# First attention and first mixture of a two-layer gated block: earlier start of block 0, ternary halves one step later, a written-out ending, 23 tiles and weight loads in pieces

## The reference, cut to what matters

```python
x = x + tanh(g_xattn[0]) * xattn0(layernorm(x), ctx, ctx)   # 16 heads of 16, softmax over 128 keys
x = x + tanh(g_ffn[0]) * ffn0(layernorm(x))
# xattn0: q = x Wq + bq; k = ctx Wk + bk; v = ctx Wv + bv; softmax(q k / 4) v Wo + bo
# ffn0: weights replaced by sign * row mean of |W| where |W| > half of that mean, else 0
#   shared expert:  silu(h sw1^T) sw2^T
#   routed expert:  the one of 8 experts with the largest router probability, times that probability
```

## Time and profile before

| | |
|---|---|
| median of three runs | 1084.05 us |
| the profiled execution, its own time | 1094.73 us |
| its span from the first to the last instruction | 1093.0 us |
| mean granted TensorE clock over the span | 0.938 |
| PE, DVE, ACT, POOL busy | 89%, 71%, 56%, 21% of the span |
| first attention | 0 to 210.7 us |
| routing and shared expert | 210.9 to 282.2 us |
| expert tiles | 282.5 to 363.2 us |
| second layer | from 363.3 us to the end |

### The profile page before, as it was taken

One profiled execution on the slowest core, in us unless ns is written; L12 is line 12 of the kernel. 1 busy time (PEld: TensorE's weight loads), 2 busy tenths in 40 slices (PEclk: granted clock), 3 DMA queues, 4 the chain that ended last, 5 costly groups with the idle time before them and its releaser, 6 DMA issues. The chain is left out here.

```text
span 1093.0 us, 22464 instructions
## 1 busy us (share of the span) xinstructions
PE 972.3 (89%) x8152; PEld 900.7 (82%) x8152; DVE 770.8 (71%) x1924; ACT 609.9 (56%) x1460; POOL 229.9 (21%) x289
## 2 busy tenths in 40 slices
PE   3899999777798579999999999999979999799992
PEld 2788887677687468999999999999968999698991
DVE  5788887664576677878777767766776777465655
ACT  3477775374597545555555555555537444565650
POOL 3534443005000342010100000010000000466631
PEclk9799998778899879999999999999999999899996
DMA  8511110002264220000000000003014000444417
GB/s 273 180 60 41 60 60 2 1 9 69 89 192 110 61 64 1 20 14 8 21 1 20 2 20 1 21 1 97 1 60 135 1 2 6 126 130 136 139 56 260
DMA packets 66044, 69.67 MB, mean 64 GB/s; under 512 B 14352, under 2 KB 56848, under 8 KB 65808
## 3 DMA queue, kind: packets, MB, share of 16 engines
q1 hardware_dynamic: 59440, 53.28, 16.0%
q0 software_dynamic: 5376, 14.69, 4.6%
q10 hardware_dynamic: 1120, 0.27, 0.1%
HBM read 46.20 MB, written 22.02 MB: 62 GB/s over the span
## 5 line engine op out<-in xcount | busy, mean ns | idle before, releaser
L1452 PE MATMUL a_psK<-a_kvThi,a_wk 128*128 128x512 f32 x256 | 97.4, 421 | 4.9 <-issue 2.6
L309 POOL TENSOR_SCALAR t_neg<-t_raw,t_nthr 128x256 bf16<-128x256 f32 (+1 forms) x54 | 60.7, 1138 | 108.0 <-DVE t_nthr L507 108.0
L1511 PE MATMUL a_psY<-a_nwhi,a_uhi 128*128 128x256 f32 x256 | 73.8, 288 | 5.1 <-DVE a_ulo L1684 5.1
L1571 ACT ACTIVATE a_probs<-a_psS,a_softmax 128x256 f32<-128x256 f32 x128 | 59.5, 470 | 29.8 <-DVE a_softmax L1666 29.0
L1492 PE MATMUL a_psU<-a_pThi,a_tokhi 128*128 128x256 f32 x256 | 72.4, 283 | 0.0
L1492 PE MATMUL a_psU<-a_pTlo,a_tokhi 128*128 128x256 f32 x256 | 72.4, 283 | 0.0
L1492 PE MATMUL a_psU<-a_pThi,a_toklo 128*128 128x256 f32 x256 | 72.4, 283 | 0.0
L1511 PE MATMUL a_psY<-a_nwlo,a_uhi 128*128 128x256 f32 x256 | 72.3, 282 | 0.0
L1511 PE MATMUL a_psY<-a_nwhi,a_ulo 128*128 128x256 f32 x256 | 72.2, 282 | 0.0
L1561 ACT ACTIVATE a_khi<-a_psK,a_bk 128x512 fp32r<-128x512 f32 x64 | 44.0, 688 | 50.2 <-PE a_psK L1452 49.6
L1583 ACT ACTIVATE a_uhi<-a_psU 128x512 fp32r<-128x512 f32 x64 | 38.2, 597 | 58.9 <-PE a_psU L1492 58.8
(11 more groups left out here) (385 smaller groups left out, 3229.4 us busy)
## 6 DMA issues: line engine op xcount, KB each, us to landing
t_raw<-in_L_ffn_expert_w SPq DMA_DIRECT2D x16, 512.0 KB, 3.8
f_raw<-in_fc_T SPq DMA_DIRECT2D x16, 512.0 KB
m_results<-a_zeros SPq DMA_DIRECT2D x8, 512.0 KB
m_sorted<-m_zeros SPq DMA_DIRECT2D x1, 3072.0 KB, 11.8
e_xin<-m_sorted SPq DMA_DIRECT2D x24, 128.0 KB, 2.9
m_expert_out<-e_y SPq DMA_DIRECT2D x24, 128.0 KB, 1.9
a_rawkv<-in_L_xattn_Wkv SPq DMA_DIRECT2D x2, 1024.0 KB, 6.4
m_n<-in_sh_T SPq DMA_DIRECT2D x2, 1024.0 KB, 7.7
```

The lines of the kernel that those rows point to most:

```text
L309: ins = pool.tensor_scalar(neg[:, own], raw[h % NRAW][:, own], nthr[h % 2][:, n:n + 1], None, ALU.is_lt)
L1452: ins = pe.matmul(psK[:].rearrange("p b t -> p (b t)"), wk[x][:, a, h * DH:(h + 1) * DH], kvT[pair % 2][y][:, a, :, :, :].rearrange("p b m ...
L1511: ins = pe.matmul(psY[:, b, :], u[ch % 2][x][:, f, hh * P:(hh + 1) * P], nw[y][:, f, 2 * j + hh, :], start=first, stop=last, skip_group_ch ...
L1571: act.activation(probs[n % 2][:, b, :], psS[n % 2][:, b, :], ACT.Exp, bias=nmax[:, n % NM, b:b + 1], accum_out=sums[:, n % NM, b:b + 1]).t ...
```

## The change

It does five things.

1. Loads at the start: Wk comes ahead of Wq, and x part 1 ahead of half 0, context part 1 ahead of half 1. Each weight has a semaphore of its own.
2. Block 0: PE turns its context alone (`first_context`), and makes its values and keys, before its normed rows are there; the queries follow (`first_queries`) into another accumulator (a_psT). DVE makes the normed rows of block 1 before `entry(1)`.
3. Halves: PE turns half h in step h, not h - 1; DVE's `signs`, POOL's `below` and ACT's `magnitudes` and `keep` move by one step as well.
4. The last four steps of PE are a written list (`ending`), with the second transposed scores of a block ahead of the weighing.
5. Mixture: NT is 23, the most tiles that 2048 tokens in 8 groups can fill. The first three tiles are loaded into rows of n_sb while the shared expert is still computed, by SP inside the block of `front_0`. The weights come in 16 pieces of 256 KB, one in each of the steps 1 to 16, and the small parameters in step 17.

```diff
+def most_tiles(blocks, experts):
+    return (blocks * P + experts * (P - 1)) // P
...
-                for n, key in (("v", "Wv"), ("q", "Wq"), ("k", "Wk")):
+                for n, key in (("v", "Wv"), ("k", "Wk"), ("q", "Wq")):
                     load_w(n, key)
+                load_x(1)
                 load_raw(0)
+                load_ctx(1)
                 load_raw(1)
-                load_x(1)
-                load_ctx(1)
                 load_raw(2)
...
-                    if due(t + 2):
-                        below(t + 2)
+                    if due(t + 1):
+                        below(t + 1)
...
+                def first_context():
+                    act.wait_ge(s["c0_turned"], 1)
+                    act.activation(xcT[0][:, 2:4, :], psX[:, 2:4, :], ACT.Copy).then_inc(s["c0_out"], 1)
...
+                    if t >= -1 and due(t + 2):
+                        magnitudes(t + 2)
+                    if NB - 1 <= t <= NB:
+                        exps(t - 1, 1)
+                    if t == NB - 1:
+                        maxima(t)
+                    if due(t):
+                        keep(t)
...
+                    if t == -2:
                         entry(1)
+                    if t == 1:
+                        signs(1)
                     if there(t):
                         maximum(t, 1)
                         split(t)
-                    if due(t + 2):
-                        signs(t + 2)
-                    if t == -1:
+                    if t == 0:
+                        magnitudes(1)
+                        signs(0)
+                    if t >= 1 and due(t + 1):
+                        signs(t + 1)
+                    if t == 0:
                         dve.wait_ge(s["gates_done"], 1)
...
-                    if due(t + 3):
-                        magnitudes(t + 3)
+                    if t >= 0 and due(t + 2):
+                        magnitudes(t + 2)
...
+                def first_context():
+                    pe.wait_ge(s["c_in0"], 16)
+                    for a in range(KD):
+                        ins = pe.transpose(psX[:, 2 + a, :], ctx_sb[:, 0, a * P:(a + 1) * P], ident[:])
+                    ins.then_inc(s["c0_turned"], 1)
+                    pe.wait_ge(s["c0_out"], 1)
+                    pe.wait_ge(s["w_inv"], 16)
+                    value(0)
+                    pe.wait_ge(s["w_ink"], 16)
...
-                    if due(t + 1):
-                        turn_half(t + 1)
+                    if due(t):
+                        turn_half(t)
                     scores(t + 1, 0, t - 1, 1)
...
+                def ending():
+                    turn_maxima(NB - 2)
+                    scores(NB - 1, 1, NB - 2, 0)
+                    output(NB - 4)
+                    scores(NB, 0, NB - 2, 1)
+                    spread(NB - 1)
+                    turn_maxima(NB - 1)
+                    weigh(NB - 3)
+                    turn_half(NB - 1)
+                    scores(NB, 1, NB - 1, 0)
+                    output(NB - 3)
+                    weigh(NB - 2)
+                    scores(NB, 1, NB - 1, 1)
+                    turn_half(NB)
+                    output(NB - 2)
+                    weigh(NB - 1)
+                    turn_half(NB + 1)
+                    spread(NB + 1)
+                    output(NB - 1)
...
-    NT = NB + NE
+    NT = most_tiles(NB, NE)
...
+        def first_tiles(sp):
+            for n in range(2):
+                sp.wait_ge(scattered[n], NB // 2 * 16)
+            for j in range(EARLY):
+                sp.dma_start(xin[j][:], xg.rearrange("(t p) d -> t p d", p=P)[j]).then_inc(x_in[j], 16)
...
-                    if t in (4, 8, 12, 16):
-                        load_weights(t // 4 - 1)
-                    if t == 18:
+                    if 0 <= t - WEIGHTS_FROM < len(pieces):
+                        load_weights(t - WEIGHTS_FROM)
+                    if t == WEIGHTS_FROM + len(pieces):
                         load_small()
```

More of the change, by code:

```diff
@@ L387, in step @@
                 def step(t):
-                    if there(t - 1):
+                    if there(t - 1) and t < NB:
                         maxima(t - 1)
-                    if due(t) and half(t)[1] == 1:
-                        keep_scale(t)
+                    if due(t - 1) and half(t - 1)[1] == 1:
+                        keep_scale(t - 1)
                     if there(t + 1):
@@ L576, in value, with first_queries @@
+                def first_queries():
+                    pe.wait_ge(s["txc_done"], 1)
+                    pe.wait_ge(s["w_inq"], 16)
+                    for m in range(2):
+                        for a in range(KD):
+                            ins = pe.matmul(psT[0][:, m, :], W["q"][:, a, m * P:(m + 1) * P], xcT[0][:, a, :], start=(a == 0), stop=(a == KD - 1))
+                    ins.then_inc(s["qk_done"], 1)
                 def value(i):
-                    pe.wait_ge(s["txc_done"], i + 1)
@@ L688, in step @@
                 def step(t):
-                    if due(t) and half(t)[1] == 1:
-                        spread(t)
+                    if due(t - 1) and half(t - 1)[1] == 1:
+                        spread(t - 1)
                     if there(t - 1):
                         turn_maxima(t - 1)
-                    if there(t + 1):
+                    if t == -1:
+                        first_queries()
+                    elif there(t + 1):
                         value(t + 1)
@@ L702, in step @@
                         weigh(t - 2)
-                    if due(t + 1):
-                        turn_half(t + 1)
+                    if due(t):
+                        turn_half(t)
                     scores(t + 1, 0, t - 1, 1)
-                steps(step)
+                def ending():
[17 more added lines that the diff above has]
+                    output(NB - 1)
+                first_context()
+                for t in range(-2, NB - 1):
+                    step(t)
+                ending()
 def prefix_steps(dve, s, src, bufs, n):
@@ L795, in front_0, with _ @@
         with nc.Block() as block:
+            @block.sync
+            def _(sp):
+                first_tiles(sp)
             @block.gpsimd
@@ L1047, in expert_tiles @@
         s = {n: sem(f"e0_{n}", c) for n in names}
[L1048 removed]
+        y_out = [s["out0"], s["out1"]]
+        WEIGHTS_FROM, PIECE = 1, D
+        pieces = [(n, i) for n, key in (("kv", "L1_xattn_Wkv"), ("q", "L1_xattn_Wq")) for i in range(A[key].shape[1] // PIECE)]
+        pieces += [("o", i) for i in range(A["L1_xattn_Wo"].shape[0] // (2 * P))]
+        assert WEIGHTS_FROM + len(pieces) < NT
         LAG_UP, LAG_TURN2, LAG_DOWN, LAG_OUT = 2, 4, 6, 7
@@ L1064, in _ @@
             def _(sp):
-                for n in range(2):
-                    sp.wait_ge(scattered[n], NB // 2 * 16)
                 def load(j):
@@ L1099, in load_small @@
                             sp.dma_start(dst, src).then_inc(loaded["small"], 16)
-                for j in range(NIN - 1):
-                    load(j)
+                assert loaded_before == NIN - 1
                 def step(t):
```

129 lines of the change are left out of this document (76 added, 53 removed).

## The result

| | before | changed |
|---|---|---|
| median of 20 runs each, us | 1089.22 (1076.66 to 1094.84) | 1078.47 (1066.92 to 1085.26) |
| ratio, 95% interval | | 0.9908 (0.9879 to 0.9938) |
| span of the profiled execution | 1093.0 | 1077.2 |
| mean granted clock over the span | 0.938 | 0.941 |
| end of the first attention | 210.75 | 204.70 |

The changed kernel is 10.75 us, 0.9%, faster. The medians are those of all twenty runs; the ratio is of the means of those within 1.5% of each kernel's fastest. Measured twice more, with the kernel before beside it each time, it came out at 0.9839 (0.9778 to 0.9900) and 0.9928 (0.9893 to 0.9964). The profiled pair differs by 15.8 us, but 5.9 of these lie in the second layer, whose code is the same; the first layer gives 9.9.

A forecast was written before the change was run, and what follows sets the result against it. PE, busy throughout from 80 to 179.4 us, was taken as the bound, leaving gains at the edges. Terms -11.2 + 1.0 - 2.0 - 2.6 - 0.5 = -15.3 us from the median 1084.05 gave 1068.8 us, range 1058 to 1081.

The forecast's parts named there:

- the 1% on which I had put 0.67: Whole kernel: chance 0.67 of measuring faster, below 1073.2 us, since a measurement can tell about 1% (10.8 us).
- Start, -11.2: First attention's start: scores waiting for block 1's maxima begin at 31.3 instead of 42.54; -11.2 us, bounds -7.5 and -13.1.
- The claim that nothing is lost between: Between start and end, from step 1 on: each engine does the same per step, only for another half; nothing lost.
- Ending, +1.0: First attention's end: 29.5 us from the start of the last scores against 28.5 before; +1.0 us, bounds -3.4 and +4.5.
- T + 27.7: First attention's end at full clock, 27.7 us after T, the start of the last scores.
- DVE's wait for POOL: First attention's end: DVE waits for POOL before the last signs; PE idles over 4 us; hiding DVE's 2.6 bounds -3.4.
- Early load, -2.0: Tiles' start: first load issued some 15 us earlier, so PE starts behind the barrier; -2.0 us, bounds 0 and -3.6.
- One tile, -2.6: Expert tiles: one tile less, 2.65 us each, all on PE; -2.6 us, at least -1.7.
- Pieces, -0.5: Tiles' weight loads: 256 KB pieces take back some waiting for stores; -0.5 us, bounds -3.4 and +8.8.
- Rivals 1 and 2: Tiles: pieces hold up stores, +29.6 us, chance 0.07; or pieces mildly rate-limited, +8.8 us, chance 0.07.
- The small loads stay: Tiles: the burst of small loads stays, one tile earlier; its 3.46 us on PE and 6.2 on DVE not removed.
- Rival 3: First attention: low clock makes the start -7.5 and the ending +4.5 us, giving 1076.0 us; chance 0.18.

The follow-up runs named there:

- small_early: Changed kernel with the eight small parameter loads issued by SP at the start of the routing stage, not in step 17; 0.9801 of before.
- weigh_first: Changed kernel with block 13 weighed ahead of block 14's second transposed scores and block 15's maxima, as before the change; 0.9843 of before.
- generic_end: Changed kernel with PE's ordinary step to the last one in place of the written ending, ACT's order matched; 0.9871 of before.
- signs_late: Changed kernel with DVE's signs(17) and the norm steps moved behind heads_out(14); 0.9847 of before.
- tiles24: Changed kernel with NT set to 24 tiles; 0.9977 of before.
- weights_1mb: Changed kernel with the weights in four loads of 1 MB in steps 4, 8, 12 and 16; 0.9913 of before.
- attn_only: Kernel before with the first attention of the changed one, mixture left as before; 0.9947 of before.
- mix_only: Changed kernel with the first attention of the kernel before, new mixture kept; 0.9975 of before.
- both_late: Changed kernel with block 13 weighed early on PE, and signs(17) and norm steps behind heads_out(14) on DVE; 0.9822 of before.
- best: Changed kernel with block 13 weighed early, signs(17) and norm steps behind heads_out(14), small loads in the routing stage; 0.9839 of before, measured again 0.9817.
- generic_late_small: Changed kernel with ordinary steps to the end, signs(17) and norm steps behind heads_out(14), small loads in the routing stage; 0.9843 of before.
- before_again: Kernel before, unedited, profiled once more; its first attention ended 28.6 us after the start of the last scores.

## Why the prediction was right in part

The time, 1078.47 us, lies inside the range of 1058 to 1081, 9.7 us above the forecast. The change was forecast at -15.3 us and measured at -10.75, and at -0.9% it fell just on the other side of the 1% on which I had put 0.67. Of the 9.7, 4.5 are this size, and 5.2 are the kernel before, whose median over 20 runs is 1089.22 where three had 1084.05.

- **Start, -11.2: right.** 31.24 was measured for 31.3, and 14.20 for the first scores where 15.2 was said. At T it was -12.1 in both pairs of profiles. The claim that nothing is lost between was wrong in the small: one step took 12.9 us, with DVE's wait for POOL ahead of it and the clock at half in it; in small_early, where the clock stayed up, the same step took 10.5. But the kernel before lost more, 12.5, 10.9 and 10.6 in three steps at the low clock. In the one profile in which its clock stayed up, T was 178.43, and the start is then worth 6.6 to 9.2 us against the seven profiles of the new one, 9.2 against small_early, whose clock stayed up there as well. So about 3 of the 12.1 us are the slow clock of the kernel before, which the forecast had only in its bounds, 7.5 and 13.1. Steady steps are 10.0 and 9.8 us in turn in both kernels (`value` at 130.64, 140.64 and 150.44 before, at 128.51, 138.51 and 148.31 now); the prediction read one of the two, and the shift costs nothing in them.
- **Ending, +1.0: the step that failed.** Measured +6.1, outside the bound of +4.5. The step reads "`heads_out(13)` ends at about T + 10, as before". It ends at T + 14.3, since the list puts 8 matmuls of transposed scores, the 8 that bring in their maxima, a spread and a turning ahead of the weighing: 3.6 us (174.86 to 178.45), all at half clock. The order in the document shows this very move; I counted it as work put into gaps and not as delay of the weighing. The rest of the chain was sized at 19.5 us and took 20.3. weigh_first, which undoes this one thing, gives 5.5 us, and generic_end, which undoes the whole list, 5.3. With the clock up the prediction's T + 27.7 was near (28.3 in small_early), but the kernel before then has 23.8 and not 28.5: the sum compared an ending worked out at a middle clock with one measured with two slow stretches in it, and the new order is the slower one either way, by 4.5 or 6.1 us.
- **DVE's wait for POOL: right.** It is there with 2.57 us, PE idle for 5.09 in place of "over 4". signs_late shows it was worth 5.0, not the 2.6 that my bound allowed for hiding it: signs (1.4 us) and norm steps (2.6) go out of the path with it, while `residual(13)` stays in.
- **Early load, -2.0: right.** PE's wait of 3.64 went to 1.51, 2.1 us.
- **One tile, -2.6: right.** 2.4 by tiles24, with the reserve given there.
- **Pieces, -0.5: not contradicted, and too small to be shown.** weights_1mb gives 0.5, which is less than the scatter of that stage. Rivals 1 and 2 fell: stores land in 2.1 us. The Trainium skill (DMA: Bandwidth & Descriptors, Measured (HBM→SBUF, 128 partitions, SWDGE, issued from GpSimd)), which wants transfers of 1 MiB or more, did not decide here, since no one waited for these loads; the runs show no cost of the pieces.
- **The small loads stay: right in kind, off in size.** 3.46 us of PE's idle became 6.13. In all profiles it is 3.4 to 4.4 with the tiles of before and 4.0 to 6.1 with the new ones. Why it grew was not settled; the pieces are not the cause.
- **Rival 3** (start -7.5, ending +4.5) named the right place for the loss but put its price too low, 4.5 us against 6.1, and the smaller gain at the start that it joined to it did not come in the measured pair.

The sum with the measured terms, -12.1 + 6.1 for the attention, -2.7 for the front with the early load, -1.2 for the tiles with the grown stall, is the -9.9 of the first pair of profiles.

## What to carry to other kernels

When a list moves work of the bounding engine into a gap, look up what then stands behind it, and size that delay at the clock of that stretch: here one weighing three places later cost 5.5 us, with the longer slow stretch that came with it, nearly half of what the new start had won. An order that is fine in the steady part, where POOL's compare ends before DVE takes up the signs (at 93.12, and signs at 94.47, in the changed kernel), becomes a chain at the drain, so the last steps need their own look, engine by engine. And a burst of small loads that nobody needs yet belongs where the queues are idle: moving it took 4.7 us out of the tiles, as much as all of the mixture's part of the change (143.0 us for front and tiles in attn_only, 138.4 in mix_only).

## What was not expected of the hardware

- The same ending took 34.6 or 28.3 us and the old one 28.5 or 23.8, by whether the granted clock fell to half within a microsecond of T, the end of the 2.2 us in which PE waited ahead of the last scores. That wait is in all of them. Seven profiles have the changed attention unedited: in five the ending took 34.6 us, in one 33.2, in one 28.3. The first stretch at half clock went with the order too: it lasted about 14 us in the five and in signs_late, and 10 in the one of 33.2 (tiles24), but about 7 in both profiles of the kernel before, weigh_first, generic_end, both_late, best and generic_late_small, which all weigh block 13 early. Over the 20 runs of the changed kernel the time goes with the mean clock in the main: 1066.9 us at 0.951, 1082.0 at 0.943. Which execution keeps the clock, no run here explains.
- The first comparison and the group of before_again ran at a higher level, on the kernel before by some 20 us. There the profiles show waits in the routing stage for something remote and for issue, of 3.4 to 7.5 us in all; no profile of the other groups shows one over 1 us on PE, ACT or DVE. These are waits of the changed kernel's first profile:

```profile
ACT s_g L998 <- remote: 6.1, 2, 5.4
ACT L998 <- remote: 4.7, 1, 4.7
PE s_psY L944 <- issue: 4.3, 1, 4.3
```

The front took 70 to 74 us in the four profiles of the two kernels there, 68 in both_late and small_early, and 60 to 65 us in the other groups, for the same instructions. What is fetched from where was not tried.
